# Second-norm averages sent in batches by SyncE, first taps through GpSimd's queue, and a new order at the start of a convolve-and-rotate kernel

## The chip, the core and the metric

The kernel runs on one core of a Trainium2 chip. The metric is the time of one execution on the device in microseconds (us). The engines are TensorE (PE, its weight loads PEld), VectorE (DVE), ScalarE (ACT), GpSimd (POOL) and SyncE (SP, which here only waits and issues DMAs). A "q" behind a name (ACTq, SPq) is that engine's instruction queue while it issues a DMA.

## What is computed

The input x is 16 images of 128 channels by 64x64, float32. Two layers follow each other, each added to its input:

```python
def _gn(v, G=32, eps=1e-05):
    g = v.reshape(B_, G, C_ // G, H_, W_)
    m = jnp.mean(g, axis=(2, 3, 4), keepdims=True)
    s = jnp.var(g, axis=(2, 3, 4), keepdims=True)
    return ((g - m) / jnp.sqrt(s + eps)).reshape(v.shape)
...
x = x + _L0_conv_ref(_gn(x), L0_conv_weight)      # depthwise 5x5, 16 of 25 taps from a 3x3 weight
x = x + _L1_conv_ref(_gn(x), L1_conv_rota_matrix) # einsum('hvc,bchw->bvhw', R, feats): a 128x128 matrix for each image row
```

A norm group is four channels of one image. The second layer needs the averages of the first layer's sum over whole groups, so it can start only when the first is done.

## The kernel before

**Convolution stage.** The work goes in 32 groups of four channels (GC = 4), each group with all 16 images. A group's x sits in SBUF with image rows on the partitions (rows 0 to 63 twice, for images 0 to 7 and 8 to 15), in a ring of seven buffers (`xin`). SP loads it with eight DMAs of 128 KB. The depthwise convolution is a product with banded matrices: for each channel and each of five column shifts, GpSimd writes a band matrix into `taps` (`spread_taps`, L268: four instructions for a group) from a mask and from `row_taps`, a table of the taps spread over the partitions. That table comes from the weights by way of DRAM: DVE writes `line`, a DMA stores it to `tap_rows`, and DMAs with repeated reads bring it back (`load_taps`, L181; part 0 for groups 0 to 3, part 1 for the other 28).

All engines run hand-written loops over steps s = -3 to 34, each in a fixed order, held together by semaphores. What one group passes through, with its lines:

- DVE measures the group's x (`bn_stats`, L449, four instructions). PE averages over the partitions with small matmuls (`average_mean` L498, `average_spread` L490), DVE and ACT make scale and offset of it (`dev`, `dev2`, `spread`, `std` L355, then the reciprocal L419 and `affine` L421).
- GpSimd normalises five of eight images into `padded` (L286), ACT the other three (L360).
- PE convolves in two halves ("pairs") of two channels, 40 matmuls each (L481). The pair order of step s is: pair 0 with `average_spread(s + 1)` behind its first shift, then pair 1 with `average_mean(s + 2)` behind its first shift. The latter waits for the affine of round s + 1.
- ACT evicts each pair from PSUM into `y` (L344, four instructions), DVE adds x (L411), DVE measures the sum for the second norm (L428), and ACT stores it to `x1_scratch` in DRAM (L327, two DMAs).
- The sum's averages go through the same small chain one group in four steps later (a "round" r holds the first norm of group r and the second norm of group r - 4). In each step ACT then sends the second norm of one group from `affine` to `norm2`, the table with channels on the partitions (`send_norms`, L333, two DMAs of four runs of 64 bytes).

ACT's order in step s is evict(s-1, pair 1), std(s+1), normalise(s+1), evict(s, pair 0), store(s-1), send_norms(s-3). DVE's is affine(s+1), add(s-1, pair 1), measure the sum s-1, spread(s+2), add(s, pair 0), measure x of group s+3. GpSimd's is spread_taps(s+2), normalise(s+1). SP issues the loads of group s+5 once group s-2 has been added.

**Rotation stage.** Thirty-two granules (four image rows by eight images, 1 MB) are loaded back with channels on the partitions (L206), normalised by ACT (L379) and GpSimd (L302) with `norm2`, multiplied (L537), added by DVE (L460) and stored (L224). The first five granules are loaded in two parts, channels of groups 0 to 27 as soon as these are stored, and the last 16 channels at the end of the convolution. Granules 5 and 6 come whole behind them. ACT and GpSimd wait for all 64 sends of `norm2`.

Of the kernel before, what the change touches and what calls it, by code (L numbers as in the profile page):

```python
# [11 lines left out]
GC = 4  # L12
# [24 lines left out]
ROUNDS = GROUPS + 4  # L37
POOL_J = 5
# [17 lines left out]
def conv_rotate_kernel(nc, x, weight, rota, out):  # L56
    tap_rows = nc.dram_tensor("tap_rows", (2 * TAPS, C, KW), F32, kind="Internal").ap()
    x1_dram = nc.dram_tensor("x1_scratch", (C, H, B, W), F32, kind="Internal").ap()
    rota_src = rota.rearrange("h v c -> v h c")

    with ExitStack() as ctx:
# [62 lines left out]
        taps_landed = [sem(f"taps_landed{n}") for n in range(3)]  # L124
# [15 lines left out]
        x1_stored = [sem(f"x1_stored{n}") for n in range(YRING)]  # L140
        norm2_landed = sem("norm2_landed")
# [22 lines left out]

        def is_round(r):
            return 0 <= r < ROUNDS

        STEPS = range(-3, GROUPS + 3)

        def load_half(queue, k, n):  # L170
            for c in range(GC):
                queue.dma_start(xin[k % XRING][n * HALF:(n + 1) * HALF, :, c],  # L172
                                x[n * J:(n + 1) * J, k * GC + c].rearrange("j h w -> h j w")
                                ).then_inc(x_landed[k % XRING], 16)

# [11 lines left out]
        def _(sp):  # L187
            for k in range(XRING - 1):
                load_half(sp, k, 0)
                if k >= 3:  # L190
                    load_half(sp, k, 1)

            for s in range(GROUPS + 3):
                if group(s + XRING - 2) and s >= 1:
                    if s >= 2:
                        sp.wait_ge(x1_ready, 2 * (s - 1))
                    load_half(sp, s + XRING - 2, 0)
                    load_half(sp, s + XRING - 2, 1)
                if s in range(ROT_STEP, ROT_STEP + ROT_LOADS):
                    n = s - ROT_STEP  # L200
                    rows = slice(n * (H // ROT_LOADS), (n + 1) * (H // ROT_LOADS))
                    sp.dma_start(rot_all[:, rows], rota_src[:, rows]).then_inc(rot_landed, 16)
# [23 lines left out]

            for n in range(EARLY, IRING):
# [9 lines left out]
        def _(pool):  # L237
# [10 lines left out]
            for d in range(TAPS):  # L248
                pool.wait_ge(near_ready, d + 1)
                nc.gpsimd.affine_select(out=near[:], in_=near[:], compare_op=ALU.not_equal, fill=1.0, base=d - PAD,  # L250
                                        pattern=[[-1, HALF + BAND]], channel_multiplier=1).then_inc(near_ready, 1)
            pool.wait_ge(line_stored[0], 32)
            load_taps(pool, 0, 1, taps_landed[1])
            pool.wait_ge(mask_ready, 2)

            def spread_taps(k):
                if k < FIRST:
                    pool.wait_ge(taps_landed[0], 16 * TAPS)
                    pool.wait_ge(taps_landed[1], 16 * TAPS)
                else:  # L260
                    pool.wait_ge(taps_landed[2], 16 * 2 * TAPS)
# [15 lines left out]
            for s in STEPS:  # L277
                if group(s + 2):
# [29 lines left out]
        def _(act):  # L308
# [5 lines left out]
            for part, cs in enumerate((slice(0, FIRST * GC), slice(FIRST * GC, C))):  # L314
                for n in range(2):
                    act.dma_start(tap_rows[n * TAPS:(n + 1) * TAPS, cs].rearrange("r c k -> c r k"),
                                  line[cs].rearrange("c (r k) -> c r k", r=TAPS)).then_inc(line_stored[part], 16)
            load_half(act, 1, 1)
            act.wait_ge(line_stored[0], 32)
            load_taps(act, 0, 0, taps_landed[0])  # L320
# [15 lines left out]
            def evict(k, pair):  # L336
                bank = 2 * ((2 * k + pair) % PAIRS)
                act.wait_ge(convolved, 2 * k + pair + 1)
                if pair == 0 and k >= YRING:
                    act.wait_ge(x1_stored[k % YRING], 32 * (k // YRING))  # L340
                    act.wait_ge(stats_ready, k - YRING + 5)
# [6 lines left out]
            for s in STEPS:  # L348
# [20 lines left out]
                if group(s - 3):  # L369
# [3 lines left out]
            act.wait_ge(norm2_landed, 32 * GROUPS)  # L373
# [17 lines left out]
        def _(dve):  # L391
# [21 lines left out]

            for s in STEPS:
                if is_round(s + 1):
# [8 lines left out]
                if group(s - 1):  # L424
                    add(s - 1, 1)
                    dve.wait_ge(x1_ready, 2 * s)
                    for q in range(J // 2):
                        last = nc.vector.bn_stats(  # L428
                            out=stats[:, (s + 3) % 2, 1, 2 * q:2 * q + 2].rearrange("p j f -> p (j f)"),
                            in_=y[(s - 1) % YRING][:, :, 2 * q:2 * q + 2].rearrange("p c j w -> p c w j"))  # L430
# [14 lines left out]
                if group(s + 3):  # L445
                    k = s + 3
                    dve.wait_ge(x_landed[k % XRING], 16 * 2 * GC * (k // XRING + 1))
                    for q in range(J // 2):
                        last = nc.vector.bn_stats(  # L449
                            out=stats[:, k % 2, 0, 2 * q:2 * q + 2].rearrange("p j f -> p (j f)"),  # L450
                            in_=xin[k % XRING][:, 2 * q:2 * q + 2].rearrange("p j c w -> p (c w) j"))
                if is_round(s + 3):
                    last.then_inc(stats_ready, 1)
# [11 lines left out]
        def _(pe):  # L465
# [27 lines left out]
            def average_mean(r, half):  # L493
                k = norms(r)
                pe.wait_ge(stats_ready, r + 1)
# [70 lines left out]
```

## Time and profile before

| | us |
|---|---|
| median of 3 runs | 543.72 (543.0 to 543.99) |
| the profiled execution, its own time | 545.81 |
| span of its trace | 544.0 |
| TensorE busy | 423.9 (78% of the span) |
| VectorE busy | 348.4 (64%) |
| GpSimd busy | 334.5 (61%) |
| ScalarE busy | 299.7 (55%) |

The mean TensorE clock was 0.972 of full speed. The shares are means over two stages with different limits: the convolution up to about 355 us, in which PE, DVE and GpSimd are busy nearly all the time, and the rotation from about 377 us, in which the DMA engines are. DMA moved 140.67 MB.

### The profile page before, as it was taken

The numbers are of one execution on the slowest core, as the hardware profiler recorded it, in microseconds if no ns is written. First come the engines' busy times: TensorE is split into PE (matmuls) and PEld (weight loads), VectorE is DVE, ScalarE is ACT, GpSimd is POOL, SyncE is SP. The second block draws the span as 40 slices with busy tenths as digits, with TensorE's granted clock in tenths as the row PEclk, the third lists the DMA queues.
The fourth block names the chain that finished last, engine by engine and source line by source line (L and its number), as shares of the span: only waits on it lengthen the run. The fifth ranks groups of instructions, "written<-read, shape, count | busy, mean of one in ns | idle before, by whom it ended". The sixth has DMA issues, their size and how long they took to land.

```text
span 544.0 us, 8852 instructions
## 1 busy us (share of the span) xinstructions
PE 423.9 (78%) x3168; PEld 201.9 (37%) x3168; DVE 348.4 (64%) x648; ACT 299.7 (55%) x566; POOL 334.5 (61%) x416
## 2 busy tenths in 40 slices
PE   0048999989989989989989989911999867676772
PEld 0024554434444444444434444511444323233230
DVE  3226988778878878878869787740674444535353
ACT  1116666566566567566567677623677455454640
POOL 4299788878888888988889986202344323232320
PEclk9999999999999999999999999975899999999997
DMA  9998998988888988987889998958599999999998
GB/s 142 182 199 143 242 221 201 217 196 201 218 203 197 218 205 196 226 207 194 218 198 262 270 268 228 360 128 204 167 371 396 393 397 397 395 397 396 398 391 302
DMA packets 208170, 140.67 MB, mean 259 GB/s; under 512 B 140096, under 2 KB 172928, under 8 KB 208128
## 3 DMA queue, kind: packets, MB, share of 16 engines
q1 hardware_dynamic: 181200, 103.31, 68.8%
q10 hardware_dynamic: 26128, 35.28, 24.7%
q0 software_dynamic: 800, 1.54, 1.3%
q8 instruction: 25, 0.41, 0.3%
q14 instruction: 17, 0.14, 0.1%
HBM read 72.95 MB, written 67.13 MB: 258 GB/s over the span
## 4 chain that ended last, share of the span: by engine, by line
ACT 24%; ACTq 21%; DMA 17%; PE 13%; issue 8%; SPq 8%; DVE 5%; POOL 2%; DVEq 0%; POOLq 0%
ACT area L344 17%; DMA out_dram<-area 15%; ACTq L333 14%; PE ps L481 8%; SPq L206 7%; ACT area L360 5%; PE ps L537 4%; ACTq L327 4%; ACT std L355 2%; DVE affine L419 1%; DMA norm<-affine 1%; POOL area L268 1%; SPq L224 1%; ACTq L172 1%; DMA row_taps<-tap_rows 1%
## 5 line engine op out<-in xcount | busy, mean ns | idle before, releaser
L481 PE MATMUL ps<-area 64*64 64x512 f32 x2560 | 295.3, 601 | 13.7 <-POOL area L286 11.5
L344 ACT ACTIVATE area<-ps 64x512 f32<-64x512 f32 x256 | 150.8, 589 | 95.2 <-issue 79.5
L481 PEld LDWEIGHTS ps<-area 64*64 64x64 f32 x2560 | 138.6, 132 | 120.6 <-issue 120.6
L268 POOL TENSOR_TENSOR area<-mask,row_taps 128x325 f32<-128x325 f32 x128 | 158.0, 1267 | 23.9 <-PE ps L481 14.0
L537 PE MATMUL ps<-area 128*128 128x512 f32 x256 | 120.1, 610 | 38.9 <-DVE area L460 29.3
L460 DVE TENSOR_TENSOR area<-ps,area 128x512 f32<-128x512 f32 x128 | 81.5, 685 | 84.7 <-DMA out_dram<-area 64.9
L302 POOL TENSOR_SCALAR area<-area,norm 128x256 f32<-128x256 f32 x96 | 52.0, 555 | 130.3 <-PE ps L537 78.6
L286 POOL TENSOR_SCALAR area<-area,affine 128x256 f32<-128x256 f32 x160 | 113.0, 719 | 29.9 <-DVE affine L421 29.9
L379 ACT ACTIVATE area<-area,norm 128x256 f32<-128x256 f32 x160 | 82.0, 588 | 69.2 <-PE ps L537 47.5
L449 DVE BATCH_NORM_STATS2 stats<-area 128x6 f32<-128x512 f32 x128 | 80.6, 692 | 15.7 <-DMA area<-in_x_dram 15.7
L537 PEld LDWEIGHTS ps<-area 128*128 128x128 f32 x256 | 46.4, 193 | 101.4 <-DVE area L460 53.7
L428 DVE BATCH_NORM_STATS2 stats<-area 128x6 f32<-128x512 f32 x128 | 80.7, 694 | 1.1
L411 DVE TENSOR_TENSOR area<-area 128x1024 f32<-128x1024 f32 x64 | 79.9, 1249 | 0.0
L360 ACT ACTIVATE area<-area,affine 128x256 f32<-128x256 f32 x96 | 50.7, 592 | 17.4 <-DVE affine L421 17.4
L498 PE MATMUL ps<-stats,half_mean 64*64 64x16 f32 (+1 forms) x144 | 17.1, 200 | 50.9 <-DVE affine L421 40.0
L419 DVE RECIPROCAL affine<-std 128x16 f32<-128x16 f32 (+1 forms) x36 | 8.7, 241 | 72.2 <-ACT std L355 72.2
L498 PEld LDWEIGHTS ps<-stats,half_mean 64*64 64x64 f32 x144 | 16.4, 137 | 76.0 <-issue 66.1
L355 ACT ACTIVATE std<-ps,eps 128x16 f32<-128x16 f32 (+1 forms) x36 | 9.8, 272 | 44.6 <-issue 25.4
L490 PEld LDWEIGHTS ps<-spread,half_mean 64*64 64x64 f32 x144 | 18.6, 140 | 23.6 <-issue 12.2
L490 PE MATMUL ps<-spread,half_mean 64*64 64x16 f32 (+1 forms) x144 | 16.5, 197 | 5.0 <-DVE spread L440 5.0
L181 POOL DMA_DIRECT2D row_taps<-tap_rows x15 | 8.8, 592 | 6.3 <-DMA tap_rows<-line 6.3
L523 PEld LDWEIGHTS ps<-ident,rot_all 128*128 128x128 f32 x64 | 8.2, 146 | 9.0 <-issue 9.0
(23 smaller groups left out, 51.6 us busy)
## 6 DMA issues: line engine op xcount, KB each, us to landing
x_scratch<-area ACTq DMA_DIRECT2D x64, 512.0 KB, 6.5
out_dram<-area SPq DMA_DIRECT2D x32, 1024.0 KB, 11.4
area<-in_x_dram SPq DMA_DIRECT2D x244, 128.0 KB, 4.2
area<-x_scratch SPq DMA_DIRECT2D x27, 1024.0 KB, 12.6
area<-x_scratch SPq DMA_DIRECT2D x5, 896.0 KB, 11.5
area<-in_x_dram ACTq DMA_DIRECT2D x12, 128.0 KB, 7.1
row_taps<-tap_rows POOLq DMA_DIRECT2D x8, 142.2 KB, 6.5
norm<-affine ACTq DMA_DIRECT2D x64, 0.2 KB
```

Source lines behind the costliest of these rows:

```text
L268: last = nc.gpsimd.tensor_tensor(taps[k % TRING][:, c * KW:(c + 1) * KW].rearrange("p d (b r) -> p d b r", r=TAPS), bass.AP(tensor=of_rows ...
L286: last = nc.gpsimd.tensor_scalar(padded[k % GRING][:, :, j, PAD:PAD + W], xin[k % XRING][:, j], affine[:, k, 0, 0, j:j + 1], affine[:, k, ...
L333: act.dma_start(norm2[k * GC:(k + 1) * GC, n], affine[n * HALF:n * HALF + GC, k + 4, 1]).then_inc(norm2_landed, 16)
L344: last = nc.scalar.activation(y[k % YRING][rows, 2 * pair + c], ps[half, bank + n].rearrange("p (j w) -> p j w", j=J), ACT.Identity)
L360: last = nc.scalar.activation(padded[k % GRING][:, :, j, PAD:PAD + W], xin[k % XRING][:, j], ACT.Identity, scale=affine[:, k, 0, 0, j:j + ...
L379: last = nc.scalar.activation(gn[n % NRING][:, :, j], tin[n % IRING][:, :, j], ACT.Identity, scale=norm2[:, n % 2, 0, j:j + 1], bias=norm2 ...
L411: nc.vector.tensor_tensor(part, part, xin[k % XRING][:, :, cs].rearrange("p j c w -> p c j w"), ALU.add).then_inc(x1_ready, 1)
L428: last = nc.vector.bn_stats(out=stats[:, (s + 3) % 2, 1, 2 * q:2 * q + 2].rearrange("p j f -> p (j f)"), in_=y[(s - 1) % YRING][:, :, 2 * ...
L449: last = nc.vector.bn_stats(out=stats[:, k % 2, 0, 2 * q:2 * q + 2].rearrange("p j f -> p (j f)"), in_=xin[k % XRING][:, 2 * q:2 * q + 2]. ...
L460: nc.vector.tensor_tensor(tout[n % ORING][:, :, h], ps[:, (n * RH + h) % 6, :].rearrange("p (j w) -> p j w", j=J), tin[n % IRING][:, h], A ...
L481: last = nc.tensor.matmul(ps[half, bank + n], taps[k % TRING][rows, (2 * pair + c) * KW + d, 0:H], padded[k % GRING][rows, 2 * pair + c, : ...
L537: nc.tensor.matmul(ps[:, m % 6, :], rot_t[u % 2][:, h], gn[n % NRING][:, h], start=True, stop=True).then_inc(rotated, 1)
```

## The change

Four things change.

1. The second-norm averages of groups 0 to 27 are no longer sent by ACT. SP writes them to a DRAM table `norm2_scratch` in four batches of seven groups (`store_norms`, two DMAs each), three inside its loop at s = 11, 18 and 25, the fourth between the loads of granules 2 and 3, and fetches the table with one DMA. ACT still sends those of groups 28 to 31. SP waits for all of `norm2` before it loads granules 5 and 6.
2. The part-0 taps are stored and loaded by GpSimd's queue alone (before: stored by ACT, one half loaded by ACT, the other by GpSimd). The part-1 taps are loaded by SP, between the x loads of groups 3 and 4 (before: by GpSimd at s = -1).
3. At s = -1 GpSimd normalises group 0 first and spreads the taps of group 1 after it.
4. From s = 4 on (FILL) DVE measures x of group s+3 at the start of step s, not at its end, so at that place two groups are measured one behind the other. The semaphore `stats_ready` now counts the two kinds of measurement apart.

```diff
+NBATCH = 7
+LAST = GROUPS - GROUPS % NBATCH
+FILL = 4
...
+        def measured(r):
+            return min(r + 1, GROUPS) + max(r - 3, 0)
...
+        NORM2 = 16 + 32 * (GROUPS - LAST)
...
         def _(sp):
+            def store_norms(first):
+                groups = slice(first, first + NBATCH)
+                sp.wait_ge(affine_ready, first + NBATCH + 4)
+                for n in range(2):
+                    sp.dma_start(norm2_dram.rearrange("(g c) n k j -> c g n (k j)", c=GC)[:, groups, n],
+                                 affine[n * HALF:n * HALF + GC, first + 4:first + 4 + NBATCH, 1].rearrange(
+                                     "p g k j -> p g (k j)")).then_inc(norm2_stored, 16)
+
             for k in range(XRING - 1):
                 load_half(sp, k, 0)
                 if k >= 3:
                     load_half(sp, k, 1)
+                if k == 3:
+                    sp.wait_ge(line_stored[1], 32)
+                    load_taps(sp, 1, 0, taps_landed[1])
+                    load_taps(sp, 1, 1, taps_landed[1])
...
                     load_half(sp, s + XRING - 2, 0)
                     load_half(sp, s + XRING - 2, 1)
+                if s > NBATCH + 3 and (s - NBATCH - 4) % NBATCH == 0 and s - NBATCH - 4 < LAST - NBATCH:
+                    store_norms(s - NBATCH - 4)
...
                 load_granule(n, early).then_inc(in_landed[n], 16)
+                if n == 2:
+                    store_norms(LAST - NBATCH)
+            sp.wait_ge(norm2_stored, 32 * (LAST // NBATCH))
+            sp.dma_start(norm2[0:LAST * GC], norm2_dram[0:LAST * GC]).then_inc(norm2_landed, 16)
...
+            sp.wait_ge(norm2_landed, NORM2)
             for n in range(EARLY, IRING):
                 load_granule(n, slice(0, C)).then_inc(in_landed[n], 16)
...
+            pool.wait_ge(line_ready, len(POS_IDX + NEG_IDX))
+            store_line(pool, 0)
             pool.wait_ge(line_stored[0], 32)
-            load_taps(pool, 0, 1, taps_landed[1])
+            load_taps(pool, 0, 0, taps_landed[0])
+            load_taps(pool, 0, 1, taps_landed[0])
...
             for s in STEPS:
-                if group(s + 2):
+                if group(s + 2) and s != -1:
                     spread_taps(s + 2)
...
                 if s == -1:
-                    pool.wait_ge(line_stored[1], 32)
-                    load_taps(pool, 1, 0, taps_landed[2])
-                    load_taps(pool, 1, 1, taps_landed[2])
-
-            pool.wait_ge(norm2_landed, 32 * GROUPS)
+                    spread_taps(1)
+
+            pool.wait_ge(norm2_landed, NORM2)
...
-                if group(s - 3):
+                if s - 3 in range(LAST, GROUPS):
                     send_norms(s - 3)
...
+            def measure(k):
+                dve.wait_ge(x_landed[k % XRING], 16 * 2 * GC * (k // XRING + 1))
+                if k >= 2:
+                    dve.wait_ge(spread_ready, k - 1)
...
             for s in STEPS:
+                if group(s + 3) and s >= FILL:
+                    measure(s + 3)
                 if is_round(s + 1):
...
                 if group(s):
                     add(s, 0)
-                if group(s + 3):
-                    k = s + 3
...
+                if group(s + 3) and s < FILL:
+                    measure(s + 3)
```

The order of the instructions on ACT, in the middle of the convolution stage (two steps, before). L344 is the eviction, L355 std, L360 the normalisation, L327 the store of the sum, L333 the sends:

```order
L344 ACTIVATE area<-ps 64x512 x4
L355 ACTIVATE std<-ps,eps 128x16
L360 ACTIVATE area<-area,affine 128x4x64 x3
L344 ACTIVATE area<-ps 64x512 x4
L327 DMA x_scratch<-area 64x4x512 x2
L333 DMA norm<-affine 4x16 x2
L344 ACTIVATE area<-ps 64x512 x4
```

The same place now (L370 eviction, L381 std, L386 normalisation, L353 store):

```order
L370 ACTIVATE area<-ps 64x512 x4
L381 ACTIVATE std<-ps,eps 128x16
L386 ACTIVATE area<-area,affine 128x4x64 x3
L370 ACTIVATE area<-ps 64x512 x4
L353 DMA x_scratch<-area 64x4x512 x2
L370 ACTIVATE area<-ps 64x512 x4
```

The two sends between the store and the next eviction are gone.

GpSimd at the start, before (L181 loads of row_taps, L268 spread_taps, L286 normalisation):

```order
L181 DMA row_taps<-tap_rows 13x5x80 x4
L181 DMA row_taps<-tap_rows 12x5x80
L268 TENSOR_TENSOR area<-mask,row_taps 128x325 x8
L286 TENSOR_SCALAR area<-area,affine 128x4x64 x5
L181 DMA row_taps<-tap_rows 13x5x560 x4
L181 DMA row_taps<-tap_rows 12x5x560
L181 DMA row_taps<-tap_rows 13x5x560 x4
L181 DMA row_taps<-tap_rows 12x5x560
L268 TENSOR_TENSOR area<-mask,row_taps 128x325 x4
L286 TENSOR_SCALAR area<-area,affine 128x4x64 x5
```

And now (L188 the store of the line, L196 loads, L301 spread_taps, L319 normalisation):

```order
L188 DMA tap_rows<-line 16x5x5 x2
L196 DMA row_taps<-tap_rows 13x5x80 x4
L196 DMA row_taps<-tap_rows 12x5x80
L196 DMA row_taps<-tap_rows 13x5x80 x4
L196 DMA row_taps<-tap_rows 12x5x80
L301 TENSOR_TENSOR area<-mask,row_taps 128x325 x4
L319 TENSOR_SCALAR area<-area,affine 128x4x64 x5
L301 TENSOR_TENSOR area<-mask,row_taps 128x325 x8
L319 TENSOR_SCALAR area<-area,affine 128x4x64 x5
```

Ahead of the first spread there are now twelve DMAs, not five. Behind it only the normalisation of group 0 stands, the ten part-1 loads have left the queue, and the spreads of groups 1 and 2 follow each other.

## Rows read from the trace of the kernel before

**Rows 1.** Head of the page: the span.

```profile
span 544.0 us, 8852 instructions
```

**Rows 2.** Waits: engine line <- releaser: us in total, times, longest.

```profile
ACT area L344 <- issue: 79.5, 26, 3.8
...
POOL area L286 <- DVE affine L421: 29.9, 26, 3.6
...
DVE stats L449 <- DMA area<-in_x_dram: 15.7, 3, 7.4
```

**Rows 3.** Timeline of ACT, one step: start, us, engine line op [idle before <-releaser].

```profile
200.02 2.44 ACT L344 ACTIVATE area<-ps 64x512 f32<-64x512 f32 x4 [3.00 <-issue]
...
206.00 1.99 ACTq L333 DMA_DIRECT2D norm<-affine  x1
...
208.01 2.15 ACTq L333 DMA_DIRECT2D norm<-affine  x1
210.21 2.44 ACT L344 ACTIVATE area<-ps 64x512 f32<-64x512 f32 x4 [3.01 <-issue]
```

**Rows 4.** Timeline of GpSimd: spreads of groups 4, 5, 19 and 31.

```profile
57.05 5.09 POOL L268 TENSOR_TENSOR area<-mask,row_taps 128x325 f32<-128x325 f32 x4 [1.62 <-PE ps L481]
...
65.93 4.05 POOL L268 TENSOR_TENSOR area<-mask,row_taps 128x325 f32<-128x325 f32 x4 [1.10 <-PE ps L481]
...
207.37 5.11 POOL L268 TENSOR_TENSOR area<-mask,row_taps 128x325 f32<-128x325 f32 x4 [0.41 <-PE ps L481]
213.54 3.60 POOL L286 TENSOR_SCALAR area<-area,affine 128x256 f32<-128x256 f32 x5 [1.06 <-DVE affine L421]
...
327.45 5.08 POOL L268 TENSOR_TENSOR area<-mask,row_taps 128x325 f32<-128x325 f32 x4 [0.43 <-PE ps L481]
```

**Rows 5.** Timelines of DVE and GpSimd, single instructions where they meet.

```profile
207.37 2.10 POOL L268 TENSOR_TENSOR area<-mask,row_taps 128x325 f32<-128x325 f32 x1 [0.41 <-PE ps L481]
...
68.97 2.09 DVE L411 TENSOR_TENSOR area<-area 128x1024 f32<-128x1024 f32 x1
...
207.34 1.22 DVE L411 TENSOR_TENSOR area<-area 128x1024 f32<-128x1024 f32 x1
208.48 2.51 DVE L449 BATCH_NORM_STATS2 stats<-area 128x6 f32<-128x512 f32 x4
212.97 0.25 DVE L419 RECIPROCAL affine<-std 128x16 f32<-128x16 f32 x1 [1.99 <-ACT std L355]
```

**Rows 6.** Timelines of GpSimd and PE, the start.

```profile
10.50 3.05 POOL L181 DMA_DIRECT2D row_taps<-tap_rows  x5 [6.30 <-DMA tap_rows<-line]
23.42 7.96 POOL L268 TENSOR_TENSOR area<-mask,row_taps 128x325 f32<-128x325 f32 x8 [9.87 <-DMA row_taps<-tap_rows]
...
34.03 5.79 POOL L181 DMA_DIRECT2D row_taps<-tap_rows  x10
...
34.17 1.98 PE L481 MATMUL ps<-area 64*64 64x512 f32 x8 [11.51 <-POOL area L286]
...
47.76 1.09 PE L481 MATMUL ps<-area 64*64 64x512 f32 x8 [2.08 <-issue]
```

**Rows 7.** Issue to landing: the row_taps loads, then SP's x loads.

```profile
DMA to landing us min/median/max: 4.7/7.1/8.1
...
DMA to landing us min/median/max: 2.6/4.2/9.8
```

**Rows 8.** Between the stages: ACT's timeline, and a window (busy us, clock, DMA share, GB/s).

```profile
368.91 1.20 ACTq L333 DMA_DIRECT2D norm<-affine  x2
376.71 2.56 ACT L379 ACTIVATE area<-area,norm 128x256 f32<-128x256 f32 x5 [8.28 <-DMA norm<-affine]
...
380.00:385.00 5.00, 5.00 (x8) 2.19 (x9) 1.76 (x3) 2.21 (x5) 0.01 (x1) 0.63 0.01 3
```

**Rows 9.** Windows of the convolution stage, the same columns.

```profile
56.00:66.00 10.00, 10.00 (x104) 5.53 (x98) 9.62 (x17) 6.65 (x13) 7.84 (x10) 1.00 1.01 228
...
200.00:240.00 40.00, 36.26 (x352) 17.49 (x348) 31.74 (x60) 25.90 (x48) 34.30 (x37) 1.00 0.87 206
```

More of the change, by code:

```diff
@@ L123, in conv_rotate_kernel @@
         mask_ready = sem("mask_ready")
-        taps_landed = [sem(f"taps_landed{n}") for n in range(3)]
+        taps_landed = [sem(f"taps_landed{n}") for n in range(2)]
         taps_ready = sem("taps_ready")
@@ L174, in load_half, with store_line @@
                                 ).then_inc(x_landed[k % XRING], 16)
+        def store_line(queue, part):
+            cs = slice(0, FIRST * GC) if part == 0 else slice(FIRST * GC, C)
+            for n in range(2):
+                queue.dma_start(tap_rows[n * TAPS:(n + 1) * TAPS, cs].rearrange("r c k -> c r k"),
+                                line[cs].rearrange("c (r k) -> c r k", r=TAPS)).then_inc(line_stored[part], 16)
         def load_taps(queue, part, n, landed):
@@ L313, in _ @@
             act.wait_ge(line_ready, len(POS_IDX + NEG_IDX))
[L314 to L317, printed above, removed]
+            store_line(act, 1)
             load_half(act, 1, 1)
-            act.wait_ge(line_stored[0], 32)
-            load_taps(act, 0, 0, taps_landed[0])
             load_half(act, 2, 1)
@@ L340, in evict @@
                     act.wait_ge(x1_stored[k % YRING], 32 * (k // YRING))
-                    act.wait_ge(stats_ready, k - YRING + 5)
+                    act.wait_ge(stats_ready, measured(k - YRING + 4))
                 low, high = slice(0, HALF), slice(HALF, P)
@@ L412, in add, with measure_sum @@
                                         ALU.add).then_inc(x1_ready, 1)
+            def measure(k):
+                dve.wait_ge(x_landed[k % XRING], 16 * 2 * GC * (k // XRING + 1))
+                if k >= 2:
+                    dve.wait_ge(spread_ready, k - 1)
+                for q in range(J // 2):
+                    last = nc.vector.bn_stats(
+                        out=stats[:, k % 2, 0, 2 * q:2 * q + 2].rearrange("p j f -> p (j f)"),
+                        in_=xin[k % XRING][:, 2 * q:2 * q + 2].rearrange("p j c w -> p (c w) j"))
+                last.then_inc(stats_ready, 1)
+            def measure_sum(k):
+                for q in range(J // 2):
+                    last = nc.vector.bn_stats(
+                        out=stats[:, (k + 4) % 2, 1, 2 * q:2 * q + 2].rearrange("p j f -> p (j f)"),
+                        in_=y[k % YRING][:, :, 2 * q:2 * q + 2].rearrange("p c j w -> p c w j"))
+                last.then_inc(stats_ready, 1)
             for s in STEPS:
+                if group(s + 3) and s >= FILL:
+                    measure(s + 3)
                 if is_round(s + 1):
@@ L426, in _ @@
                     dve.wait_ge(x1_ready, 2 * s)
[L427 to L430, printed above, removed]
+                    measure_sum(s - 1)
                 if is_round(s + 2):
@@ L494, in average_mean @@
                 k = norms(r)
-                pe.wait_ge(stats_ready, r + 1)
+                pe.wait_ge(stats_ready, measured(r))
                 if r >= 1:
```

18 lines of the change are left out of this document (5 added, 13 removed).

## The prediction, made before the changed kernel was run

> **What bounds the kernel now.** I read the waits first. ACT's evictions stood 79.5 us in 26 waits that no engine released ("issue") [rows 2]: the instruction queue itself was late. GpSimd's normalisation lost 29.9 us in 26 waits for DVE's affine, once a step. ACT's timeline of one step says what its queue did [rows 3]: it issued two sends of norm averages, 1.99 and 2.15 us, from 206.00 to 210.16, and the eviction of the finished pair started at 210.21, 10.19 us after the same eviction of the step before. PE had finished that pair by about 207.4, since GpSimd's next spread, which waits for it, began at 207.37 [rows 4]. So the eviction came some 2.8 us late. Behind it stand std (ACT, in order), then DVE's reciprocal, which had idled 1.99 us for it [rows 5], then affine, and for affine GpSimd waited 1.06 us, at 213.54, before it could normalise the next group [rows 4]. PE needs that normalised group. The loop of one step is thus sends, eviction, std, affine, normalisation, matmuls.
>
> How fast would it go otherwise? GpSimd's spreads mark the steps, since each waits for the group three before. Those of groups 4 and 5 are 8.88 us apart (57.05, 65.93), before the first send; from group 5 to group 31 it is 26 steps in 261.52 us, 10.06 each [rows 4].
>
> **The sends leave ACT (25 us).** Per step two issues (4.14 us) go. They are not 4.14 us a step on the path: the eviction can come 2.8 us sooner, affine then 2.0 us sooner at most, because DVE itself is busy until its measurement ends (10.19 - 1.99 = 8.20 us of work a step [rows 5]). Affine would be there before GpSimd ends its spread, so its 1.06 us wait goes: 10.19 - 1.06 = 9.13 us by GpSimd's own work (5.11 + 3.60 and what stands between) [rows 4]. In that time each of DVE's two adds makes one GpSimd instruction wait: the spread instruction beside the add at 207.34 took 2.10 us, where four of them took 4.05 us undisturbed, 1.01 each [rows 4, 5]. A step with only one such meeting is about 1.1 us shorter for GpSimd, and then PE's matmuls set it, at the 8.88 us seen. So the new step lies between 8.88 and, if DVE's adds are held up now and then as the one at 68.97 was (2.09 for 1.22, 0.87 us [rows 5]), about 9.5: 8.20 + 0.87 + one or two shorter waits. I take 9.1, near GpSimd's 9.13, as the row in the middle of the stage is nearer to the new state than the first steps. 26 x (10.06 - 9.1) = 25.0 us. At 8.88 it is 30.7, at 9.5 it is 14.6. The last steps before the end of the convolution still carry sends (groups 28 to 31), and stay.
>
> The batches on SP: six issues in the loop, two ahead of granule 3. At the 2.15 us of an ACT send [rows 3], the nearest row, a batch holds SP's queue 4.3 us, once in seven steps; behind it stand the x loads of the next group. These have room: a group is loaded after the add of the group seven before, and measured now some two steps and a half later (before: three and a half). Eight loads issued over one step of 9.1 us and landing 4.2 us later (9.8 at most) [rows 7] are there after 13 to 19 us, and two steps and a half are 22.8. A batch takes 4.3 of the 4 to 9.5 us left over, once. Cost 0; if that cover is gone, 1 us for each of three batches. The part-1 taps now delay the x of groups 4 and 5 on SP, by about the 5.8 us that their issue took on GpSimd [rows 6]. These groups are measured in steps 1 and 2, after 50 us, 0 again.
>
> **Measuring one group ahead (1.4 us lost).** The place in DVE's order is the same (between the last add and affine); only the group is another. It gains nothing in a step. Once, at s = 4, two measurements stand there: 2.51 us more ahead of affine [rows 5]. GpSimd needs affine when its spread ends, some 5.1 us into PE's group, and DVE could have had it at about 4.0 (208.48 + 2.51 + 0.4, counted from 207.37). So about 1.1 us is cover and 1.4 us is lost; bounds 0 and 2.5.
>
> **The start (4.9 us gained).** Part 0 of the taps: GpSimd began its first loads at 10.50, when ACT's store had landed, and the spreads at 23.42, when the slower half (ACT's) had [rows 6]. Now GpSimd stores. Its queue is free at about 4.2 us (it then waited 6.30, to 10.50). A load there takes about 0.6 us to issue (3.05 / 5) [rows 6] and 4.7 to 8.1 us to land, median 7.1 [rows 7]; a store of its own is in no row, so I price it as a load. Store issued by 5.4, landed 9.5 to 12.9, ten loads issued 5.8 us long, the last landed 19.5 to 26.2. I take medians: second store at 4.8 + 7.1 = 11.9, last load issued at 17.2, landed at 24.3, which is 0.9 us later than 23.42. After that GpSimd goes: spread 0 and normalisation 0, without the 3.98 us of spread 1 ahead (7.96 / 2), so PE starts at 34.17 + 0.9 - 4.0 = 31.1. Up to group 1's convolution, which started at 47.76, both spreads and both normalisations count as before, but the ten part-1 loads (5.79 us) are gone: 47.76 + 0.9 - 5.8 = 42.9. Group 0 on PE takes as long as before, 34.17 to 45.68 (2.08 idle before 47.76), 11.5 us: 42.6, so GpSimd still decides. 4.9 us gained; bounds 3.0 and 9.7.
>
> **Between the stages (3.5 us gained).** The last sends were issued at 368.91 and ended at 370.11, and ACT and GpSimd waited for their landing to 376.71 [rows 8], 6.6 us. Meanwhile the loads of granules 5 and 6, 2 MB, had been put into the DMA engines. Now SP holds these two back until `norm2` has landed. A landing took 2.6 us at the least and 4.2 in the middle for SP's x loads [rows 7], so the wait falls from 6.6 to 2.6 to 4.2: 2.4 to 4.0 gained, I take 3.5, because only five small loads stand ahead. The two granules then land while the DMA engines had nothing to do (share 0.01 at 380 to 385 [rows 8]); the rest of the rotation stage, paced by DMA, moves as a whole. The table's fetch by SP stands before 350 us, under the convolution.
>
> **Sum.** 544.0 [rows 1] - 25.0 + 1.4 - 4.9 - 3.5 = 512.0. The profiled execution's span is 0.3 us above the median of the runs (543.72), so 511.7; the two slow steps behind the spread of group 31 give up to 0.7 more. I say **511 us**.
>
> **A rule that speaks against it.** DVE's add and GpSimd's work excluded each other: 2.10 against 1.01 on one side, 2.09 against 1.22 on the other [rows 5]. [...] The small `dev2` and `spread` would fall under it as well. [...]
>
> **Rivals.**
> - *The lock sets the step (12 in 100).* In the profile DVE's adds started when GpSimd was waiting, because the late affine had made it wait. If both adds of a step are held up by 0.87 us each, DVE's step is 8.20 + 1.74 = 9.94 us, and the sends' removal gives 26 x 0.12 = 3.1 us; at one add and the small ones, 9.6, 12 us. Time 525 to 534, say 528. Against it: between 57 and 66 us PE lost nothing (10.00 of 10.00 busy [rows 9]) with DVE busy 9.62 of it, and adds that wait make GpSimd's gaps in which the next one is free.
> - *DMA sets the step (in the forecast's own range).* The engines were busy 0.87 of the time at 206 GB/s, and reached 228 GB/s at 1.01 [rows 9]: 10.19 x 206 / 228 = 9.2 us a step, 2.6 us less gain, 514.
> - *Slower than before (2 in 100).* DVE now waits for an x one group younger in front of affine. If x is late in every step, the loads pace everything. With the other gains (7 us) this ends above 543.7 once a step costs 10.06 + 7 / 26 = 10.3 us, i.e. once the loads and stores fall below 206 x 10.19 / 10.3 = 204 GB/s. At 200 GB/s: 10.5 us, 548. Only 15.7 us in three waits, all in the first groups, were ever spent on x [rows 2].
> - *It doesn't do what it says (1 in 100).* The issue wait is the DMA queue's fullness and moves to ACT's two stores, which stand at the same place; then only the start and the middle give 7 us, 537. Against it: the first steps, with stores and loads and without sends, were the fast ones.
>
> **Numbers.** The forecast's case, a step of 8.88 to 9.45 us, has 85 in 100: 502 to 522. To it I add the nearer part of the lock case: range 501 to 525. A difference under 0.2% (1.1 us) can't be told from none here. Faster by more 0.97, same 0.01, slower 0.02.
>
> **What would show it.** The evictions' "issue" wait gone in the middle of the stage; GpSimd's spreads 9.1 us apart; its wait for affine near 0 and DVE's wait for std well under 1 us. PE's first convolution at 31 us, the second at 43. ACT's first normalisation of the rotation stage 3 to 4 us after the last send. Wrong would be: adds of 2.1 us on DVE in most steps (lock), waits of DVE for x (DMA), or stores of 2 us on ACT's queue (fullness).

## Result: 515.9 us, 5% faster, and the profile after

| | before | after |
|---|---|---|
| median, us | 543.86 (4 runs, 543.0 to 546.19) | 515.86 (4 runs, 513.55 to 518.63) |
| ratio, 95% interval | | 0.948 [0.942, 0.954] |
| the profiled execution, its own time | 545.81 | 517.14 |
| span of its trace | 544.0 | 515.3 |

The forecast was 511, range 501 to 525. Two of experiment 9's six executions (532.9 and 663.7 us, over 1.5% above its fastest) are left out of its ratio. The head of the page after:

```profile
span 515.3 us, 8833 instructions
```

The waits after, against [rows 2] (us in total, times, longest):

```profile
ACT area L370 <- PE ps L517: 55.0, 34, 2.9
...
DVE stats L445 <- DMA area<-in_x_dram: 18.8, 4, 6.4
...
POOL area L319 <- DVE affine L467: 11.2, 3, 5.4
```

The evictions' 79.5 us of "issue" are gone: ACT now waits for PE. GpSimd's 26 waits for affine have become three. DVE's waits for x have become four, and the longest of these matters below.

GpSimd's timeline after, against [rows 4, 6] (start, us, what, idle before): the taps at the start, the spreads of groups 5 and 9, two in the middle, and those of groups 30 and 31.

```profile
14.40 5.78 POOL L196 DMA_DIRECT2D row_taps<-tap_rows  x10 [8.65 <-DMA tap_rows<-line]
26.71 4.00 POOL L301 TENSOR_TENSOR area<-mask,row_taps 128x325 f32<-128x325 f32 x4 [6.52 <-DMA row_taps<-tap_rows]
...
63.29 4.05 POOL L301 TENSOR_TENSOR area<-mask,row_taps 128x325 f32<-128x325 f32 x4 [1.10 <-PE ps L517]
...
100.13 5.42 POOL L301 TENSOR_TENSOR area<-mask,row_taps 128x325 f32<-128x325 f32 x4 [0.65 <-PE ps L517]
...
180.05 5.15 POOL L301 TENSOR_TENSOR area<-mask,row_taps 128x325 f32<-128x325 f32 x4 [0.98 <-PE ps L517]
...
188.93 4.07 POOL L301 TENSOR_TENSOR area<-mask,row_taps 128x325 f32<-128x325 f32 x4 [1.04 <-PE ps L517]
...
286.61 4.04 POOL L301 TENSOR_TENSOR area<-mask,row_taps 128x325 f32<-128x325 f32 x4 [1.04 <-PE ps L517]
296.08 3.60 POOL L319 TENSOR_SCALAR area<-area,affine 128x256 f32<-128x256 f32 x5 [5.44 <-DVE affine L467]
301.77 4.04 POOL L301 TENSOR_TENSOR area<-mask,row_taps 128x325 f32<-128x325 f32 x4 [2.09 <-PE ps L517]
```

A step is 8.88 us (180.05 to 188.93), not 10.06 and not the forecast's 9.1. Two places are longer: the four steps from 63.29 to 100.13 took 36.84 for 35.52, 1.3 us lost, and 286.61 to 301.77 is 15.16, 6.3 us lost in one step. DVE's timeline shows both, and the adds:

```profile
72.54 4.94 DVE L445 BATCH_NORM_STATS2 stats<-area 128x6 f32<-128x512 f32 x8
...
191.96 2.12 DVE L437 TENSOR_TENSOR area<-area 128x1024 f32<-128x1024 f32 x1
...
293.12 2.50 DVE L445 BATCH_NORM_STATS2 stats<-area 128x6 f32<-128x512 f32 x4 [6.40 <-DMA area<-in_x_dram]
```

The eight `bn_stats` at 72.54 are the two measurements of s = 4. At 293.12 DVE had stood 6.40 us for the x of group 31, in front of the affine for which GpSimd then waited 5.44 us. SP's timeline tells how that x came late:

```profile
256.84 0.76 SPq L231 DMA_DIRECT2D rot_all<-_L_conv_rota_matrix_dram  x1
257.64 15.89 SPq L181 DMA_DIRECT2D area<-in_x_dram  x8
273.57 0.93 SPq L207 DMA_DIRECT2D norm_scratch<-affine  x2
275.06 1.47 SPq L231 DMA_DIRECT2D rot_all<-_L_conv_rota_matrix_dram  x1
276.57 14.12 SPq L181 DMA_DIRECT2D area<-in_x_dram  x8
```

A load of rotation matrices (L231) stands ahead of the x of group 30 and another ahead of that of group 31. The eight loads of group 30 took 15.89 us to issue, a batch (L207) 0.93, the second matrix load 1.47 and the eight loads of group 31 14.12. So the queue spent 33.1 us (257.64 to 290.7) on two groups, for which PE's steps leave 17.8, and the last load was issued at 290.7; DVE went on at 293.12. ACT's timeline between the stages, against [rows 8]:

```profile
342.15 1.20 ACTq L359 DMA_DIRECT2D norm<-affine  x2
347.99 2.56 ACT L405 ACTIVATE area<-area,norm 128x256 f32<-128x256 f32 x5 [6.31 <-DMA norm<-affine]
```

PE's timeline at the start, first convolutions of groups 0 and 1, against [rows 6]:

```profile
33.50 1.99 PE L517 MATMUL ps<-area 64*64 64x512 f32 x8 [11.24 <-POOL area L319]
...
45.13 1.09 PE L517 MATMUL ps<-area 64*64 64x512 f32 x8 [0.51 <-issue]
```

And a window of the middle, against [rows 9]: PE is busy all the time (before 36.26 of 40.00), and DMA moves 244 GB/s (before 206).

```profile
240.00:280.00 40.00, 40.00 (x401) 21.50 (x397) 39.33 (x69) 28.73 (x53) 35.26 (x42) 1.00 0.99 244
```

With these rows the whole difference of the spans can be split at five places:

| stretch | before | after | difference |
|---|---|---|---|
| to the spread of group 5 | 65.93 | 63.29 | -2.6 |
| to the spread of group 31 | 261.52 | 238.48 | -23.0 |
| to the last send | 41.46 | 40.38 | -1.1 |
| to ACT's first normalisation of the rotation | 7.80 | 5.84 | -2.0 |
| to the end | 167.29 | 167.31 | 0.0 |
| sum | 544.0 | 515.3 | -28.7 |

### The profile page after: what moved, and what is told of

It reads as the page before. It is cut to its first block, busy times and chain, and to the rows that moved or that the text cites. A ratio compares the mean times of both kernels' runs of the same rounds, so it can differ in the third digit from the quotient of the medians.

```text
span 515.3 us, 8833 instructions
## 1 busy us (share of the span) xinstructions
PE 419.1 (81%) x3168; PEld 211.2 (41%) x3168; DVE 363.0 (70%) x648; ACT 299.8 (58%) x566; POOL 313.4 (61%) x413
## 4 chain that ended last, share of the span: by engine, by line
PE 48%; DMA 20%; SPq 12%; DVE 9%; POOL 3%; ACT 3%; issue 2%; ACTq 2%; DVEq 0%; POOLq 0%
PE ps L517 44%; DMA out_dram<-area 15%; SPq L235 8%; PE ps L573 3%; DVE stats L445 2%; SPq L181 2%; DVE stats L452 2%; DVE area L437 2%; DMA tap_rows<-line 2%; ACT area L370 2%; SPq L257 2%; DMA row_taps<-tap_rows 1%; ACTq L359 1%; DVE area L496 1%; POOL row_taps L196 1%
## 5 line engine op out<-in xcount | busy, mean ns | idle before, releaser
L517 PE MATMUL ps<-area 64*64 64x512 f32 x2560 | 289.1, 601 | 11.8 <-POOL area L319 11.2
L517 PEld LDWEIGHTS ps<-area 64*64 64x64 f32 x2560 | 145.0, 133 | 111.8 <-issue 111.3
L370 ACT ACTIVATE area<-ps 64x512 f32<-64x512 f32 x256 | 150.9, 589 | 59.7 <-PE ps L517 55.0
L301 POOL TENSOR_TENSOR area<-mask,row_taps 128x325 f32<-128x325 f32 x128 | 154.2, 1238 | 34.4 <-PE ps L517 27.9
L573 PE MATMUL ps<-area 128*128 128x512 f32 x256 | 121.7, 617 | 35.4 <-DVE area L496 27.8
L333 POOL TENSOR_SCALAR area<-area,norm 128x256 f32<-128x256 f32 x96 | 52.0, 555 | 128.3 <-PE ps L573 93.0
L319 POOL TENSOR_SCALAR area<-area,affine 128x256 f32<-128x256 f32 x160 | 97.9, 624 | 11.2 <-DVE affine L467 11.2
L437 DVE TENSOR_TENSOR area<-area 128x1024 f32<-128x1024 f32 x64 | 86.4, 1349 | 0.0
L386 ACT ACTIVATE area<-area,affine 128x256 f32<-128x256 f32 x96 | 50.8, 592 | 31.2 <-DVE affine L467 31.2
L534 PEld LDWEIGHTS ps<-stats,half_mean 64*64 64x64 f32 x144 | 18.4, 140 | 50.0 <-issue 35.3
L381 ACT ACTIVATE std<-ps,eps 128x16 f32<-128x16 f32 (+1 forms) x36 | 9.8, 272 | 39.5 <-issue 22.2
L483 DVE SCALAR_TENSOR_TENSOR spread<-stats,dev 128x16 f32<-128x16 f32 (+1 forms) x36 | 12.8, 356 | 1.2
## 6 DMA issues: line engine op xcount, KB each, us to landing
x_scratch<-area ACTq DMA_DIRECT2D x64, 512.0 KB, 6.1
area<-x_scratch SPq DMA_DIRECT2D x5, 896.0 KB, 10.2
```

Source lines behind the costliest of these rows:

```text
L301: last = nc.gpsimd.tensor_tensor(taps[k % TRING][:, c * KW:(c + 1) * KW].rearrange("p d (b r) -> p d b r", r=TAPS), bass.AP(tensor=of_rows ...
L319: last = nc.gpsimd.tensor_scalar(padded[k % GRING][:, :, j, PAD:PAD + W], xin[k % XRING][:, j], affine[:, k, 0, 0, j:j + 1], affine[:, k, ...
L333: last = nc.gpsimd.tensor_scalar(gn[n % NRING][:, :, j], tin[n % IRING][:, :, j], norm2[:, n % 2, 0, j:j + 1], norm2[:, n % 2, 1, j:j + 1] ...
L370: last = nc.scalar.activation(y[k % YRING][rows, 2 * pair + c], ps[half, bank + n].rearrange("p (j w) -> p j w", j=J), ACT.Identity)
L386: last = nc.scalar.activation(padded[k % GRING][:, :, j, PAD:PAD + W], xin[k % XRING][:, j], ACT.Identity, scale=affine[:, k, 0, 0, j:j + ...
L437: nc.vector.tensor_tensor(part, part, xin[k % XRING][:, :, cs].rearrange("p j c w -> p c j w"), ALU.add).then_inc(x1_ready, 1)
```

## Experiments

Medians are of 4 to 9 runs. Each ratio is against the kernel before, run on the same chip beside it. My theory after reading the two traces: the sends on ACT were the whole of the step's excess over PE's 8.88 us; early measurement brings nothing and costs the 6.3 us of group 31 and the 1.4 us of s = 4.

### 1. The sends of all groups back on ACT

The changed kernel, with no batches:

```diff
-                if s - 3 in range(LAST, GROUPS):
+                if group(s - 3):
                     send_norms(s - 3)
...
-                    store_norms(s - NBATCH - 4)
...
-                    store_norms(LAST - NBATCH)
```

> The changed kernel with ACT sending every group's averages again; batches gone, everything else as changed. My theory (the two sends in ACT's queue delay the eviction, and that paces a step): steps go back from 8.88 to about 10.1 us, ACT's issue waits are back near 80 us. 26 steps x 1.2 = 31 us more, less the 6.3 us for which DVE waited for the x of group 31 at step 28 and the 1.4 us of step 4, which slower steps hide: 540 to 542 us. Rival (the new place of the measurement gave the shorter step, the sends were free): stays at 514 to 518 us.

Measured: 539.1 us, ratio 0.991 [0.988, 0.995]. The evictions' wait is back, and the steps are 10.23 us (203.96 to 214.19 in GpSimd's spreads). Waits, then GpSimd's timeline:

```profile
ACT area L364 <- issue: 74.9, 25, 3.9
```

```profile
203.96 5.12 POOL L295 TENSOR_TENSOR area<-mask,row_taps 128x325 f32<-128x325 f32 x4 [0.40 <-PE ps L511]
...
214.19 5.10 POOL L295 TENSOR_TENSOR area<-mask,row_taps 128x325 f32<-128x325 f32 x4 [0.41 <-PE ps L511]
```

All the rest of the change is worth 5.2 us by the medians on that chip (544.3 for the kernel before), 3 to 6 by the ratio's interval. Measuring early doesn't shorten a step that the sends set.

### 2. The batches alone

The kernel before, with `store_norms` and its two places added and ACT's sends cut to groups 28 to 31 (the start, the measurement's place and the loads of granules 5 and 6 as before):

```diff
+                if s > NBATCH + 3 and (s - NBATCH - 4) % NBATCH == 0 and s - NBATCH - 4 < LAST - NBATCH:
+                    store_norms(s - NBATCH - 4)
...
+                if n == 2:
+                    store_norms(LAST - NBATCH)
...
-                if group(s - 3):
+                if s - 3 in range(LAST, GROUPS):
                     send_norms(s - 3)
```

> The kernel before with part 1 of the change alone: batches on SP, but no holding back of granules 5 and 6, old start, old place of the measurement. My theory: steps of 8.88 us and no wait for the x of group 31, 544 - 26 x 1.18 = 513 us; the start stays at 47.8 us for group 1's convolution and the wait for the last sends at 6 to 7 us. Rival (without the measurement ahead, DVE and GpSimd hold each other up, 9.1 to 9.5 us a step): 519 to 530 us.

Measured: 514.4 us, ratio 0.946 [0.941, 0.952]. This one part does as much as the whole change. By the traces (spans 511.5 and 515.3) the changed kernel gains 3.7 us on it up to the spread of group 5 (63.29 for 66.99) and 1.9 between the stages, and loses 7.6 in the steps that early measurement made long. The other 1.8 us that it is behind lie in the last steps and the rotation stage, and are not explained here.

### 3. Measuring x at the end of every step, as before

The changed kernel with one number changed:

```diff
-FILL = 4
+FILL = GROUPS + 9
```

> The changed kernel with the measurement of x at the end of the step as before (FILL beyond the last step). My theory: step 28 loses its 6.3 us, since x of group 31 is wanted some 9 us later than it is now and lands before that, and steps 4 and 5 lose their 1.4 us: 507 to 509 us, all steps 8.88. Rival (the measurement ahead is what keeps DVE in time): steps of 9.1 us or more, 514 us and above.

Measured: 506.9 us (506.65 to 508.92), ratio 0.933 [0.929, 0.937], the fastest kernel here within what can be told apart. GpSimd's timeline, the spreads of groups 5 and 31; DVE's, the measurement of group 31; and ACT's:

```profile
62.33 4.05 POOL L301 TENSOR_TENSOR area<-mask,row_taps 128x325 f32<-128x325 f32 x4 [1.11 <-PE ps L517]
...
293.20 5.17 POOL L301 TENSOR_TENSOR area<-mask,row_taps 128x325 f32<-128x325 f32 x4 [0.95 <-PE ps L517]
```

```profile
293.33 2.52 DVE L445 BATCH_NORM_STATS2 stats<-area 128x6 f32<-128x512 f32 x4
```

```profile
332.64 1.20 ACTq L359 DMA_DIRECT2D norm<-affine  x2
338.53 2.56 ACT L405 ACTIVATE area<-area,norm 128x256 f32<-128x256 f32 x5 [6.36 <-DMA norm<-affine]
```

From group 5 to 31 it is 230.87 us, 26 x 8.88 exactly: PE's floor in every step. Group 31 was measured at 293.33 without a wait. Its loads had been as slow (the eight issues took 14.04 us from 273.79); measured 8.9 us later, at the end of the step (GpSimd's spread of group 30 had begun at 284.32), they weren't late.

### 4. The rotation matrices loaded three steps later

The changed kernel with `ROT_STEP = GROUPS - 5` for `GROUPS - 8`, so that SP loads the matrices behind the last x:

> The changed kernel with the four loads of the rotation matrices issued at steps 27 to 30, behind the x of group 31, not at 24 to 27. My theory (these 4 MB ahead of the last two groups make x of group 31 late): x of group 31 lands at 280 us or sooner, the wait at step 28 goes, 509 to 510 us; step 4's 1.4 us stays. Rival (x is late because the DMA engines can't keep 8.88 us a step anyway): the wait stays above 3 us, 513 us or more.

Measured: 509.1 us, ratio 0.936 [0.932, 0.940]. The long step is gone. SP's timeline: the eight loads of group 31 now take 9.00 us, not 14.12.

```profile
265.58 4.25 SPq L207 DMA_DIRECT2D norm_scratch<-affine  x2
269.88 9.00 SPq L181 DMA_DIRECT2D area<-in_x_dram  x8
```

Here the batch took 4.25 us to issue and still no step grew: the cover that the prediction counted on was there for it.

### 5. Edits 3 and 4 together

> late_measure and rot_late together: x of group s+3 is measured at the end of step s as before the change, and SP loads the rotation matrices in steps 27 to 30. Theory, both took the same loss away in step 28 (a measurement that waited for a late x), and late_measure alone has every step at 8.88 us: together they give no more than late_measure, 506.9 within 1 us, and no step is longer than 9.0. Rival, the matrix loads still cost something in late_measure, hidden in the steps' sum or in the last steps: 504 to 505.5.

Measured: 507.6 us, ratio 0.932 [0.929, 0.935], the same as edit 3 alone (0.933). Both take the same loss away.

### 6. The order at s = -1 as before

Edit 3, and group 1's taps spread ahead of group 0's normalisation:

```diff
-                if group(s + 2) and s != -1:
+                if group(s + 2):
...
-                if s == -1:
-                    spread_taps(1)
```

> late_measure with the order at s = -1 as before the change: GpSimd spreads the taps of groups 0 and 1, then normalises group 0. The first taps still go through GpSimd's queue alone and the part-1 taps through SP. Theory, the new order only moves one spread of 4.0 us from ahead of group 0's matmuls to behind them: PE's first convolution starts 4.0 us later (about 37 for 33.0), but GpSimd has the same work to do before group 1's matmuls in either order, so group 1's convolution starts where it did (44.1) or, if PE's 11.2 us for group 0 then count, at 48: PE needs about 11.2 us from the first matmul of group 0 to the first of group 1, so 37.0 + 11.2 = 48.2, 4.1 us later, and the time is 511. Rival, GpSimd's work sets group 1's start: conv of group 1 at 44.1 to 45.5 and the time within 1.5 us of late_measure's 506.9.

Measured: 512.3 us, ratio 0.941 [0.937, 0.944]; against experiment 5 on the same chip, which also has the matrices' loads late, 4.7 us more. GpSimd's and PE's timelines:

```profile
26.73 7.96 POOL L301 TENSOR_TENSOR area<-mask,row_taps 128x325 f32<-128x325 f32 x8 [6.41 <-DMA row_taps<-tap_rows]
...
42.08 2.70 POOL L319 TENSOR_SCALAR area<-area,affine 128x256 f32<-128x256 f32 x5 [0.72 <-DVE affine L464]
```

```profile
37.48 1.98 PE L514 MATMUL ps<-area 64*64 64x512 f32 x8 [15.33 <-POOL area L319]
```

GpSimd had group 1 normalised at 44.8, but PE, which had begun 4.5 us later than in experiment 3 (32.98), came to it only at 48.0. Once the ten part-1 loads are out of GpSimd's queue, PE's own 10.5 us for group 0 set group 1's start, and the order is worth its 4 us.

### 7. The taps' store back on ACT

Edit 3, and `store_line(act, 0)` on ACT for `store_line(pool, 0)` on GpSimd:

> The changed kernel with the measurement of x at the end of the step (506.9 us, the base of this and the next three) and with ACT storing part 0 of the taps, GpSimd only loading it. My theory (what made the start later than forecast is the landing of GpSimd's own store, 8.9 us after its issue): the store lands at 9 to 10.5 us instead of 14.1, the first spread starts at 22 to 23 us instead of 26.7, group 1's convolution at 40 to 41 instead of 44.1, 3 to 4 us less in all, 503 to 504. Rival (the ten loads in one queue are the slow part, the DMA engines are full of x): first spread at 25 us or later, within 1 us of the base.

Measured: 506.5 us, ratio 0.929 [0.924, 0.934]: no difference from edit 3 that can be told. GpSimd's timeline:

```profile
12.39 5.94 POOL L196 DMA_DIRECT2D row_taps<-tap_rows  x10 [8.16 <-DMA tap_rows<-line]
25.06 4.01 POOL L299 TENSOR_TENSOR area<-mask,row_taps 128x325 f32<-128x325 f32 x4 [6.73 <-DMA row_taps<-tap_rows]
```

The loads behind the store began at 12.39, not at the 10.50 of [rows 6], and the spreads at 25.06, for 13.85 and 26.20 in experiment 3. The 3 us that I expected weren't there. The same store in experiment 2, where ACT's code up to it is that of before, let the loads start at 13.07: the 10.50 of [rows 6] is the earliest of three traces with the store on ACT.

### 8. Granules 5 and 6 not held back

Edit 3, without SP's wait:

```diff
-            sp.wait_ge(norm2_landed, NORM2)
```

> The base without SP's wait for the averages ahead of granules 5 and 6. My theory: from the last send's issue to ACT's first normalisation it takes 6.5 to 7.5 us again instead of 5.9, so 1 to 2 us more, 508 to 509. Rival (holding back is worth nothing, the sends wait for something else): the same time.

Measured: 510.1 us, ratio 0.937 [0.932, 0.942]. ACT's timeline:

```profile
332.98 1.24 ACTq L358 DMA_DIRECT2D norm<-affine  x2
341.08 2.56 ACT L404 ACTIVATE area<-area,norm 128x256 f32<-128x256 f32 x5 [8.56 <-DMA norm<-affine]
```

From the last send to the normalisation 8.10 us, against 5.89 with the hold (332.64 to 338.53): the hold is worth 2.2 us there, and 2.5 by the medians against experiment 10 (507.5, the time of experiment 3), on the same chip.

### 9. One send per group on SP, no batches

Edit 3, with SP sending each group of 0 to 27 in its loop behind the x loads:

```diff
-                    store_norms(s - NBATCH - 4)
+                if s - 5 in range(LAST):
+                    send_single(s - 5)
```

> The base with SP sending the averages of groups 0 to 27 one by one, straight to their table, two small DMAs in each step, and no batches. My theory (what counted was ACT's queue, SP's has room): steps stay at 8.88 us, time within 1.5 us of the base. Rival (batching is what pays, small sends fill the DMA queue wherever they stand): x loads come late, DVE waits for them, steps above 9.1, 513 us or more.

Measured: 527.8 us, ratio 0.967 [0.961, 0.974]. My theory fell: some 20 us slower than with batches (507.5 in experiment 10 on the same chip). Waits, then SP's timeline:

```profile
DVE stats L447 <- DMA area<-in_x_dram: 34.8, 9, 6.5
```

```profile
253.21 8.04 SPq L181 DMA_DIRECT2D area<-in_x_dram  x8
261.29 2.19 SPq L214 DMA_DIRECT2D norm<-affine  x2
263.52 9.03 SPq L181 DMA_DIRECT2D area<-in_x_dram  x8
```

SP's queue is full: 8.04 + 2.19 and two short gaps are 10.3 us for a step that PE does in 8.88, and from the first pair of sends (87.42) to the twentieth (281.76) a round takes 10.23 us in the mean, with under 5 us of waits for DVE in all. X comes late in nine waits instead of three. The queue had little room before: in experiment 3 it spent 62.66 us on the 56 loads of seven groups (from 139.18), 8.95 a group with its waits, so the loads' issues nearly fill a step even without sends. Whether the sends delay x by their own issue time alone, or also by making the loads' issues wait longer, was not separated. With the batches no stretch of SP's queue holds more than one set of sends in seven steps.

### 10. The last sends on SP as well

Edit 3, with the sends of groups 28 to 30 issued by SP before it waits for the last stores, and that of group 31 behind the five late loads:

> The base with SP sending the averages of groups 28 to 31 too, so that ACT sends none. My theory: the 4.0 us for which two sends (325.4 to 329.4) held up the std of round 34 go, and the last ones land as before: ACT's first normalisation of the rotation stage comes 3 to 5 us sooner after the last convolution, 502 to 504 us. Rival (the sends on SP come behind its waits for the last stores and land later): no gain or 1 to 2 us more.

Measured: 507.5 us, ratio 0.933 [0.928, 0.937], no difference. SP's and ACT's timelines:

```profile
330.44 2.21 SPq L241 DMA_DIRECT2D area<-x_scratch  x5
332.70 1.24 SPq L214 DMA_DIRECT2D norm<-affine  x2
```

```profile
338.20 2.56 ACT L412 ACTIVATE area<-area,norm 128x256 f32<-128x256 f32 x5 [8.06 <-DMA norm<-affine]
```

ACT's next-to-last std came 2.0 us sooner (327.43 for 329.47), but the last send stood behind the late loads and was issued at 332.70, where ACT had issued it at 332.64. That group's send from ACT with the others on SP was not tried.

## Why the prediction was right, and where it was not

The forecast lay 4.9 us below the median (0.9%). By its steps:

- **The sends leave ACT (25 us): the mechanism right, the size too small.** The evictions' "issue" wait is gone, and experiments 1 and 2 show that this part alone sets the step: 10.2 with the sends, 8.88 without. The step went to the lower bound, so the term is 261.52 - 26 x 8.88 = 30.6, 5.6 more than forecast. I had taken 9.1 because each step would hold two meetings of adds and GpSimd. PE was 40.00 of 40.00 us busy instead. The meetings exist (the add at 191.96 took 2.12 us, the one before it 1.21), but they fell into the 0.8 to 1.2 us that GpSimd now waits for PE in a step. I had added a held-up time to GpSimd's chain without asking which engine had become last.
- **"It gains nothing in a step" and "1.4 us lost": right.** Around step 4 it was 1.3 us, and experiment 3 took them away.
- **"Cost 0" for x: the failed step.** I counted 13 to 19 us from eight issues "over one step of 9.1 us" and a landing, against 22.8 of room. Near the end of the loop the matrices' loads share SP's queue, and the eight issues took 15.89 us for group 30 and 14.12 for group 31. The last load of group 31 was issued at 290.7, in experiment 4 at 278.9: 6.7 of these 11.8 us were lost before its first load and 5.1 in its own issues. Measured a step's length earlier than before, it was 6.4 us late. I had listed the x loads, the batches and the taps as SP's work, and left the matrix loads at s = 24 to 27 out. The loss needs both: experiment 3 removes it by the later measurement, 4 by the moved loads, and 5 shows that they are one.
- **The batches on SP, cost 0: right.** Three issues of a batch took 0.93, 0.87 and 4.25 us (after and experiments 3 and 4), and in experiments 3 and 4 no step shows them. In the changed kernel the 0.93 us stood in the queue ahead of the late group 31, so up to that much of its 6.3 us may be the batch's. The low cost is a property of batches, not of SP: one send a group there cost some 20 us (experiment 9).
- **The start (4.9 us gained): 2.6.** The second store from GpSimd's queue was issued at 5.2 and landed 8.9 us later (the longest by the view of its line, median 8.2), where I had taken 4.8 and, priced as a load, 7.1; first loads at 14.40, not 11.9, and the spread at 26.71 for 24.3. From there the order did as said, PE at 33.50 for 31.1. "GpSimd still decides" held by half a microsecond only: in experiment 6 PE decides. That ACT's store had landed early in the kernel before (loads at 10.50, in experiment 2 at 13.07) made no difference: its spreads waited for the slower half of the loads, and began at 23.42, in experiment 2 at 22.96. Against experiment 2, whose spread of group 5 stood at 66.99, the new start of experiment 3 (62.33) gains 4.7 us. Some 1.7 us of that 4.7 is TensorE's clock, which experiment 2 lost there (last section).
- **Between the stages (3.5 us gained): 2.0.** The landing after the last send's issue took 4.6 us (347.99 - 343.35), just outside the 2.6 to 4.2 of the x loads' rows. The hold works as described (8.10 us without it in experiment 8, 5.89 with it in experiment 3).
- **The last steps: 1.1 gained**, where I allowed 0.7 and left it out of the sum. The rotation stage didn't change.

Sum with measured terms: -30.6 (261.52 to 26 x 8.88) + 1.3 + 6.3 - 2.6 - 1.1 - 2.0 = -28.7, the difference of the spans. Against the forecast's sum for the profiled execution, 512.0, that is 3.3 us more: 6.3 lost to the late x and 2.3 + 1.5 gained less at the start and in the middle, against 5.6 + 1.1 gained more in the steps. The rest of the 4.9 us to the median is the 1.0 by which I went from 512.0 to 511, and the median's 0.6 above the span. That the total came so near is in part luck: 10.1 us of errors one way stand against 6.7 the other way.

**The rivals.** *The lock sets the step* didn't hold. Adds rose from 1249 ns in the mean before to 1349 now, and GpSimd's spreads took 5.15 or 4.07 us by turns: where the two met, one of them was held up. The spread at 180.05, with the add at 183.08 inside it (1.21 us), took 5.15 us, and the add at 191.96, begun inside the spread at 188.93 (4.07 us), took 2.12. The small `dev2` and `spread` (16 columns) rose from 193 and 199 ns in the mean to 335 and 398. It costs nothing here, with PE 40.00 of 40.00 us busy, because who is held up says nothing on whether that engine is last. *DMA sets the step* fell too: I took the 228 GB/s of one early window as the ceiling, and the same engines moved 244. In that window DVE was busy 39.33 of 40.00 us and the DMA engines 0.99 of the time, so either may be a floor close under PE's; no run tests it. *Slower than before* had its mechanism: DVE stood for an x one group younger in front of affine. It happened in one of the 25 steps that measure early (s = 4 to 28), not in all. *Moves to ACT's stores* fell: those were issued in 0.60 and 0.63 us.

```profile
194.11 0.60 ACTq L353 DMA_DIRECT2D x_scratch<-area  x1
```

## What to carry to other kernels

When a stall leaves the path, the next floor is that of the engine with the longest bare work, here PE's 8.88 us; delays of others count only past their slack to it. Room for a transfer is counted from everything in its queue, and at the worst step of the loop, not at the median one. An instruction that waits for a transfer belongs at the place where it can stand latest without delaying anyone: measuring early gave nothing and turned one slow load into a stall of the whole step.

## What the runs showed of the hardware

The longer stalls of PE cost more than their length, because the granted clock fell behind them. Windows after, around the late x of group 31 (busy us of each engine; the third figure from the end is the granted clock):

```profile
291.00:296.00 5.00, 0.75 (x8) 0.00 (x0) 2.85 (x7) 0.00 (x0) 0.00 (x0) 1.00 0.80 214
296.00:299.00 3.00, 2.88 (x22) 1.56 (x26) 2.97 (x5) 2.94 (x6) 2.92 (x4) 0.66 1.06 292
299.00:302.00 3.00, 3.00 (x28) 1.66 (x21) 2.22 (x6) 1.24 (x3) 0.91 (x3) 0.77 1.04 343
```

PE was busy 0.75 of 5.00 us, and in the 6 us behind that the clock was 0.66 and 0.77 in the mean. Of the 6.3 us of the long step, 3 x 0.34 + 3 x 0.23 = 1.7 are thus the clock, by this estimate, and 4.4 PE's wait (idle 4.37 us before 296.12); 0.2 is left over. The same happened in experiment 2 at group 1, where PE had waited 2.50 us before 47.15 and been busy 0.65 of the 3 us from 44:

```profile
47.00:50.00 3.00, 2.85 (x18) 1.23 (x22) 0.45 (x1) 0.13 (x1) 3.00 (x4) 0.61 1.02 156
50.00:53.00 3.00, 3.00 (x30) 1.68 (x26) 1.99 (x4) 1.86 (x4) 2.59 (x4) 0.83 0.60 130
```

3 x 0.39 + 3 x 0.17 = 1.7 us. From group 1's first matmul to the spread of group 4 it was 10.96 us there (47.15 to 58.11), and 9.28 after (45.13 to 54.41). In the kernel before, with 2.08 us idle at the same place [rows 6], and after, with 0.51, the clock stayed at 1.00. Experiment 9 has five more such waits. Behind PE's idle times of 2.94, 3.45 and 5.31 us (before 241.82, 318.39 and 303.68) the lowest 3 us window had a clock of 0.53, 0.55 and 0.50; behind 0.70 and 1.62 us (before 279.97 and 220.47) it stayed at 1.00. What decides was not worked out.

The store and the loads of a few KB on GpSimd's queue, while 128 KB x loads went on, took some 8 and 6 us from issue to landing, by the page after (KB each, median us):

```profile
row_taps<-tap_rows POOLq DMA_DIRECT2D x8, 20.3 KB, 5.7
...
tap_rows<-line POOLq DMA_DIRECT2D x2, 1.6 KB, 8.2
```

In nine traces of the store on GpSimd the first load behind it started between 13.74 and 14.54 us. From ACT's queue it was 10.50, 12.39 and 13.07 in three: no surer, and 1.5 us sooner where only the store's queue differed (12.39 for 13.85).

The issue of one and the same small DMA is no constant. In experiment 9 the 56 sends of 64-byte runs took from 577 to 2343 ns on SP, 652 in the middle, by the view of their tile; the eight x loads of a group took from 5.43 us there to 15.89 in the changed kernel. What sets it was not isolated here.
